# Convolution loop: one exponential instead of two, with an identity matmul that carries it to PSUM, and product buffers by step parity

## The chip, the core and the metric

The kernel runs on one core of a Trainium2 chip. The metric is the device time of one execution in microseconds (us); lower is better. The engines of the core are called TensorE (PE in the rows, its weight loads PEld), VectorE (DVE), ScalarE (ACT), GpSimd (POOL) and SyncE (SP). Each works through its own queue of instructions in order, and they meet only at semaphores.

## The reference

The whole kernel computes a convolution-like layer, then an attention layer, then a layer of experts. Only the first is touched. In it each output pixel is a sum over 49 neighbours, with weights that are a softmax over the neighbours:

```python
x1 = _conv1x1(x, w1c, b1c); x2 = _conv1x1(x, w2c, b2c); x3 = _conv1x1(x, w3c, b3c)
x2p = pad(x2, reflect)
diff = stack([x1 - x2p[:, :, dy:dy + H, dx:dx + W] for dy, dx in OFFS], axis=2)
y = relu(_bn(diff, bn1...)); y = einsum('bkln,ok->boln', y, cw1); y = relu(_bn(y, bn2...))
logits = einsum('bkln,ok->boln', y, cw2) + cw2_b
wgt = softmax(logits, axis=2)                 # over the 49 neighbours
for k, (dy, dx) in enumerate(OFFS):           # out: B, HN=8 heads, SP=8, H, W
    patch = x3p[:, :, dy:dy + H, dx:dx + W]
    out = out + patch * wgt[:, :, k]          # one weight for the 8 channels of a head
```

Shapes are B = 4 images, 64 channels, 56 x 56 pixels; the weights come from 32 channels (CR). All is float32.

## The kernel before

`conv_prepare` makes x1 and the padded x2 and x3. `conv_main`, where the change is, then works in 7 chunks of 8 rows (CH = 448 pixels). In a chunk the 49 neighbours are taken in STEPS = 14 steps of four or three neighbours (`taps`), so there are N = 98 steps. A partition of the wide tiles stands for an image, one of the (up to) four neighbours and a head.

The engines run through the same list of turns T. In one turn each engine does a piece of several steps, at fixed distances:

- POOL: `sub(T+1)` (x1 - x2 into `diff`, L411) and `shift` (logits minus their maximum, L418, in the ring `lg`), which is one step ahead of the exponentials.
- TensorE: `hidden(T)` (L596) into `ps_hid`; `sums(s-1, 1)` with s = T - 18; a rotation (L620) or the widening of the denominators (L627) in some turns; `logits(T-1)` (L611); `sums(s, 0)` (L642). `sums` adds the products of a step over its neighbours into `ps_acc`. Each product row has 448 pixels and behind them 56 columns (EXT) that hold the exponentials themselves, so that the same matmul adds up the softmax denominators.
- ScalarE: `exp_wide(s)` (L531) writes exp(logit) to the PSUM tile `ps_ev`; `front_relu(T+1)` (L510); `exp_ext(s)` (L535) computes the same 128x448 exponentials once more, into the EXT columns of the product tile (here called the edge exp); `hidden(T)` (L517); `logits(T-1)` (L522).
- VectorE: `running(T-2)` (L457, the running maximum); `product(s, 0)` and `product(s, 1)` (L477), the exponentials in `ps_ev` times the window of x3, for four channels each; `across` (L465) between the two products when a chunk's maximum is taken.

In turns T = 1 and 2 modulo 14 TensorE rotates the running maximum (L620, 128x448 against a 128*128 matrix) and the logits of that turn wait for `across`. In turns T = 4 modulo 14 ScalarE copies a finished chunk's sums out (L546, L547), and the first sums of the next chunk wait for it. In turns T = 5 modulo 14 VectorE takes the reciprocals (L493), ScalarE places them (L557), TensorE widens them (L627) and ScalarE copies the result (L564); the logits of that turn stand behind it. A turn later VectorE multiplies (L487).

`ps_ev` is one buffer: the wide exp of step s waits for `prod_done` of step s-1. The product tile `prod` is one buffer too (two halves `hs`): a product of step s waits for `acc_done` of the same half of step s-1. In the last 14 steps (s >= D0 = 84) `diff` and `ps_hid` are no longer in use, so a second product tile (`spare`) lies in `diff` and the wide exponentials rotate through the four banks of `ps_hid`, and POOL does a third of the products. SP brings a chunk's window of x3 (`win`) when the products of the chunk two before are done.

Of the kernel before, what the change touches and what calls it, by code (L numbers as in the profile page):

```python
# [26 lines left out]
NQ = 4  # L27
ROWS = 8
CH = ROWS * W
# [211 lines left out]
def conv_main(nc, x, cst, front, win, x3_dram, x3_sent, conv_out, tres_in, last_in, early_added):  # L241
    with ExitStack() as ctx:
        def sb(name, shape, dt=F32):
            return ctx.enter_context(nc.sbuf_tensor(name, shape, dt))
# [4 lines left out]
        def sem(name):  # L249
            return ctx.enter_context(nc.semaphore(name))  # L250

        QCH = CH // NQ
        EXT = QCH // 2
        ND, RING = 3, 18
        diff = sb("cm_diff", [128, ND, NQ, CH])
        hid = sb("cm_hid", [128, 2, B, CH])
        lg = sb("cm_lg", [128, RING, CH])
        prod = sb("cm_prod", [128, 2, NQ, CH + EXT])
        top = sb("cm_top", [128, 2, CH])
        topb = sb("cm_topb", [128, CH])  # L260
        rden_q = sb("cm_rden_q", [128, 2, EXT])
# [6 lines left out]
        ps_ev = psum("cm_ps_ev", [128, BANK])  # L268
# [9 lines left out]
        top_done = sem("cm_top_done")  # L278
        shift_done = sem("cm_shift_done")
        ev_done = sem("cm_ev_done")  # L280
        ext_done = sem("cm_ext_done")
        win_in = [sem(f"cm_win_in{a}") for a in range(2)]
        prod_done = sem("cm_prod_done")
# [19 lines left out]
        def mat(name, n=128):  # L303
            a = CONV_COLS[name][0]
            return cst[:, a:a + n]
# [5 lines left out]
        def step_at(T, d):  # L311

            return T - d if 0 <= T - d < N else None

        def chunk_at(T, d):
# [3 lines left out]

        D0 = N - STEPS  # L320
        SHIFTS_AHEAD = 6
        spare = diff[:, :, :, :].rearrange("p d q n -> p (d q n)")[:, 0:2 * NQ * (CH + EXT)] \
            .rearrange("p (h q n) -> p h q n", h=2, q=NQ)

        def by_pool(s, hs):

            return s >= D0 and (2 * (s - D0) + hs) % 3 == 1
# [8 lines left out]

        def halves_of(s):

            return spare if s >= D0 and (s - D0) % 2 == 0 else prod

        def wide_ev(s):

# [2 lines left out]
        def halves_free(eng, s, hs):  # L345


            if s == D0:
                eng.wait_ge(hid_done, N)
            elif s > D0:  # L350
                eng.wait_ge(acc_done, 2 * (s - 2) + hs + 1)
            elif s >= 1:
                eng.wait_ge(acc_done, 2 * (s - 1) + hs + 1)

        def window_of(s, hs):
            c, k = divmod(s, STEPS)
# [9 lines left out]
        with nc.Block() as block:  # L366
# [78 lines left out]
            @block.vector  # L445
            def _(v):
                def running(s):
                    c, k = divmod(s, STEPS)
                    v.wait_ge(logit_out, s + 1)
                    if k == 0:  # L450
                        if c >= 2:
                            v.wait_ge(rot_done, 2 * (c - 1))
                        v.tensor_scalar(top[:, c % 2, :], ps_lg[:, 0:CH], lane_bias(s), None,
                                        ALU.add).then_inc(run_done, 1)
                    else:
                        v.wait_ge(run_done, s)
                        v.scalar_tensor_tensor(out=top[:, c % 2, :], in0=ps_lg[:, 0:CH], scalar=lane_bias(s),  # L457
                                               in1=top[:, c % 2, :], op0=ALU.add, op1=ALU.max).then_inc(run_done, 1)

                def across(c, turn):  # L460

                    v.wait_ge(rot_done, 2 * c + turn + 1)
                    if turn == 1 and c >= 1:
                        v.wait_ge(shift_done, c * STEPS)
                    v.tensor_tensor(topb[:, :] if turn else top[:, c % 2, :], ps_lg[:, 0:CH], top[:, c % 2, :],  # L465
                                    ALU.max).then_inc(top_done, 1)

                def product(s, hs):
                    c, k = divmod(s, STEPS)
                    if by_pool(s, hs):  # L470
                        return
                    if k == 0 and hs == 0:
                        v.wait_ge(win_in[c % 2], 64 * (c // 2 + 1))
                    v.wait_ge(ev_done, s + 1)
                    halves_free(v, s, hs)
                    ev = wide_ev(s).unsqueeze(1).broadcast_to([128, 4, CH])
                    v.tensor_tensor(halves_of(s)[:, hs, :, 0:CH].rearrange("p s (r c) -> p s r c", c=W),  # L477
                                    ev.rearrange("p s (r c) -> p s r c", c=W), window_of(s, hs),
                                    ALU.mult).then_inc(prod_done, 1)

                v.memset(hid[96:128, 1, :, :], 0.0).then_inc(lanes_done, 1)
                v.memset(rden_d[:, :, :], 0.0).then_inc(lanes_done, 1)
                for T in TURNS:
                    c = chunk_at(T, MUL_D)
                    if c is not None:
                        v.wait_ge(wide_out, c + 1)
                        v.tensor_tensor(cout[:, :, :], cout[:, :, :],  # L487
                                        rden[:, :].unsqueeze(1).broadcast_to([128, 2, CH]),
                                        ALU.mult).then_inc(out_done, 1)
                    c = chunk_at(T, WIDE_D)  # L490
                    if c is not None:
                        v.wait_ge(acc_out, c + 1)
                        v.reciprocal(rden_q[:, :, :], rden_q[:, :, :]).then_inc(rden_done, 1)  # L493
                    if step_at(T, 2) is not None:
                        running(T - 2)
                    if step_at(T, SUM_D) is not None:
                        product(T - SUM_D, 0)
                    for turn, d in ((1, SECOND_TURN), (0, FIRST_TURN)):
                        c = chunk_at(T, d)
                        if c is not None:  # L500
                            across(c, turn)
                    if step_at(T, SUM_D) is not None:
                        product(T - SUM_D, 1)

            @block.scalar
            def _(act):
# [17 lines left out]

                def exp_wide(s):
                    act.wait_ge(shift_done, s + 1)
                    if s >= D0 + B:
                        act.wait_ge(prod_done, vector_halves(s - B, 1))
                    elif 1 <= s < D0:
                        act.wait_ge(prod_done, 2 * s)  # L530
                    act.activation(wide_ev(s), lg[:, s % RING, :], ACT.Exp).then_inc(ev_done, 1)  # L531

                def exp_ext(s):
                    halves_free(act, s, 1)
                    act.activation(halves_of(s)[:, :, :, CH:CH + EXT],  # L535
                                   lg[:, s % RING, :].rearrange("p (r h n) -> p h r n", h=2, n=EXT),
                                   ACT.Exp).then_inc(ext_done, 1)
                    if by_pool(s, 0) or by_pool(s, 1):
                        act.wait_ge(ext_done, s + 1)
                        act.activation(lg[:, s % RING, :], lg[:, s % RING, :], ACT.Exp).then_inc(flat_ev_done, 1)  # L540
# [23 lines left out]
                    act.copy(rden[:, :], ps_lg[:, 0:CH]).then_inc(wide_out, 1)  # L564

                for T in TURNS:
                    if step_at(T, SUM_D) is not None:
                        exp_wide(T - SUM_D)
                    if step_at(T, -1) is not None:
                        front_relu(T + 1)  # L570
                    c = chunk_at(T, WIDE_D)
                    if c is not None:
                        place(c)
                    if step_at(T, SUM_D) is not None:
                        exp_ext(T - SUM_D)
                    if step_at(T, 0) is not None:
                        hidden(T)
                    if c is not None:
                        widened(c)
                    c = chunk_at(T, OUT_D)  # L580
                    if c is not None:
                        sums_out(c)
                    if step_at(T, 1) is not None:
                        logits(T - 1)

            @block.tensor
            def _(pe):
# [43 lines left out]
                def sums(s, hs):  # L631
# [12 lines left out]
                                        tile_position=(0, 32 * r))  # L644
                    ins.then_inc(acc_done, 1)

                for T in TURNS:
                    if step_at(T, 0) is not None:
                        hidden(T)
                    if step_at(T, SUM_D + 1) is not None:  # L650
                        sums(T - SUM_D - 1, 1)
                    for turn, d in ((1, SECOND_TURN), (0, FIRST_TURN)):
                        c = chunk_at(T, d)
                        if c is not None:
                            rotate(c, turn)
                    c = chunk_at(T, WIDE_D)
                    if c is not None:
                        widen(c, T)
                    if step_at(T, 1) is not None:
                        logits(T - 1)  # L660
                    if step_at(T, SUM_D) is not None:
                        sums(T - SUM_D, 0)
# [1659 lines left out]
```

## Time and profile before

| | |
|---|---|
| median of 3 runs | 1947.26 us (1944.82 to 1948.8) |
| profiled execution, its own time | 1944.76 us |
| its span, first to last instruction | 1941.7 us |
| PE busy | 1695.3 us, 87% |
| DVE busy | 1198.4 us, 62% |
| ACT busy | 1176.5 us, 61% |
| POOL busy | 702.6 us, 36% |
| mean granted TensorE clock | 0.956 |

The span holds the convolution (to about 615 us), then attention, then the experts; busy shares are means over all three. In the rows a line gives the engine, the line of the kernel, the operation, the tiles written <- read and the shape; "x8" is a number of records that were merged, and the duration is then from the first one's start to the last one's end. A bracket tells how long the engine was idle before and which instruction ended it. Consecutive instructions of VectorE and ScalarE overlap by some 0.07 us in the records, so that the distance of two starts is a little less than a duration.

### The profile page before, as it was taken

The numbers are of one execution on the slowest core, as the hardware profiler recorded it, in microseconds if no ns is written. First come the engines' busy times: TensorE is split into PE (matmuls) and PEld (weight loads), VectorE is DVE, ScalarE is ACT, GpSimd is POOL, SyncE is SP. The second block draws the span as 40 slices with busy tenths as digits, with TensorE's granted clock in tenths as the row PEclk, the third lists the DMA queues.
The fourth block names the chain that finished last, engine by engine and source line by source line (L and its number), as shares of the span: only waits on it lengthen the run. The fifth ranks groups of instructions, "written<-read, shape, count | busy, mean of one in ns | idle before, by whom it ended". The sixth has DMA issues, their size and how long they took to land. (4 is left out here: it accounts for less than half of the span.)

```text
span 1941.7 us, 33831 instructions
## 1 busy us (share of the span) xinstructions
PE 1695.3 (87%) x13143; PEld 622.5 (32%) x13143; DVE 1198.4 (62%) x1798; ACT 1176.5 (61%) x1605; POOL 702.6 (36%) x401
## 2 busy tenths in 40 slices
PE   4468778778765789999999999999988999999998
PEld 1011111111111434433443443344343334433333
DVE  3239999999985576666666666666265445453433
ACT  3699999999942445454544454444464556566655
POOL 0798988988857310000000000000130114322222
PEclk9799999999987689999999999999997999999999
DMA  2121201211212210000000000100121000010000
GB/s 99 82 104 46 84 35 50 84 40 46 85 64 88 100 34 16 16 15 15 16 12 15 15 15 14 49 15 16 36 76 24 6 5 8 8 41 8 9 8 9
DMA packets 27712, 73.27 MB, mean 38 GB/s; under 512 B 6968, under 2 KB 16184, under 8 KB 26160
## 3 DMA queue, kind: packets, MB, share of 16 engines
q1 hardware_dynamic: 27280, 68.18, 11.0%
q10 hardware_dynamic: 288, 3.09, 0.4%
q8 instruction: 100, 1.64, 0.4%
q14 instruction: 44, 0.36, 0.1%
HBM read 47.84 MB, written 13.62 MB: 32 GB/s over the span
## 5 line engine op out<-in xcount | busy, mean ns | idle before, releaser
L1361 DVE TENSOR_REDUCE at_mpart<-at_ps_m 128x1 f32<-128x384 f32 (+3 forms) x800 | 396.4, 556 | 164.8 <-PE at_ps_m L1071 164.2
L1214 ACT ACTIVATE at_prob<-at_ps_s 128x896 f32<-128x896 f32 x336 | 305.0, 917 | 315.7 <-PE at_ps_s L1089 307.5
L411 POOL TENSOR_TENSOR cm_diff<-front 128x1792 f32<-128x1792 f32 x98 | 320.6, 3275 | 66.8 <-POOLq L113 37.6
L477 DVE TENSOR_TENSOR cm_prod<-cm_ps_ev,win 128x1792 f32<-128x1792 f32 x168 | 333.3, 2018 | 9.8 <-PE cm_ps_acc L642 5.2
L1906 ACT ACTIVATE ge_hid<-ge_ps,ffn 128x448 f32<-128x448 f32 x448 | 249.7, 634 | 122.6 <-PE ge_ps L1770 122.5
L1110 PE MATMUL at_ps_a<-at_prob,win 128*64 128x448 f32 x1344 | 290.0, 552 | 0.0
L1089 PE MATMUL at_ps_s<-vh,front 64*128 64x448 f16 x1344 | 252.1, 352 | 13.8 <-ACT at_prob L1214 7.8
L642 PE MATMUL cm_ps_acc<-cm_prod,cst 128*32 128x504 f32 x1456 | 200.0, 623 | 60.5 <-DVE cm_prod L477 27.0
L1089 PE MATMUL at_ps_s<-vl,front 64*128 64x448 f16 x1344 | 251.3, 351 | 0.0
L1009 POOL TENSOR_TENSOR attn<-attn 64x448 f32<-64x448 f32 x27 | 30.5, 1128 | 485.7 <-DMA attn<-attn 485.7
L1747 PE MATMUL ge_ps<-ge_hid,ffn 128*64 128x448 f32 x896 | 194.6, 555 | 0.5 <-DVE ge_part L2088 0.4
L517 ACT ACTIVATE cm_hid<-cm_ps_hid,cst 128x1792 f32<-128x1792 f32 x98 | 170.5, 1740 | 0.3 <-PE cm_ps_hid L596 0.3
L1071 PE MATMUL at_ps_m<-front,vh 64*128 64x384 f16 (+3 forms) x800 | 158.5, 338 | 10.5 <-DVE at_mpart L1361 9.0
L1770 PE MATMUL ge_ps<-attn,w1h 128*128 128x448 f16 (+1 forms) x448 | 160.9, 359 | 0.0
L1770 PE MATMUL ge_ps<-attn,w1l 128*128 128x448 f16 (+1 forms) x448 | 159.8, 357 | 0.0
L510 ACT ACTIVATE cm_diff<-cm_diff 128x1792 f32<-128x1792 f32 x98 | 147.5, 1505 | 13.7 <-POOL cm_diff L411 13.7
L596 PE MATMUL cm_ps_hid<-cm_diff,cst 32*32 32x448 f32 x2744 | 107.0, 577 | 53.5 <-ACT cm_hid L517 35.8
L2081 DVE COPY ge_wide<-ge_ps 128x448 f32<-128x448 f32 x112 | 69.9, 624 | 134.3 <-PE ge_ps L1760 133.8
L418 POOL TENSOR_TENSOR cm_lg<-cm_lg,cm_topb 128x448 f32<-128x448 f32 x98 | 115.5, 1184 | 48.8 <-DVE cm_topb L465 48.8
L2088 DVE SCALAR_TENSOR_TENSOR ge_part<-ge_ps,ffn,ge_wide 128x448 f32<-128x448 f32 x112 | 76.4, 682 | 77.5 <-PE ge_ps L1747 75.9
L2151 POOL TENSOR_TENSOR ge_total<-ge_part 128x448 f32<-128x448 f32 x28 | 32.1, 1146 | 246.9 <-DVE ge_part L2088 246.9
L1110 PEld LDWEIGHTS at_ps_a<-at_prob,win 128*64 128x64 f32 x1344 | 81.7, 136 | 122.9 <-issue 94.4
(232 smaller groups left out, 1964.4 us busy)
## 6 DMA issues: line engine op xcount, KB each, us to landing
win<-x_dram SPq DMA_DIRECT2D x28, 868.0 KB
at_rden<-rden_dram SPq DMA_DIRECT2D x27, 224.0 KB, 3.2
x_dram<-win SPq DMA_DIRECT2D x4, 962.0 KB
conv_out<-cm_cout SPq DMA_DIRECT2D x28, 112.0 KB, 3.6
win<-x SPq DMA_DIRECT2D x2, 1568.0 KB, 12.7
t_dram<-front SPq DMA_DIRECT2D x2, 1568.0 KB, 7.4
attn<-attn SPq DMA_DIRECT2D x28, 112.0 KB, 2.3
front<-t_dram SPq DMA_DIRECT2D x2, 1568.0 KB, 7.6
```

The source lines that it names most:

```text
L411: pool.tensor_tensor(diff[:, s % ND, 0:n, :].rearrange("p n (r c) -> p n r c", c=W), a.rearrange("p n (r c) -> p n r c", c=W), b, ALU.subt ...
L477: v.tensor_tensor(halves_of(s)[:, hs, :, 0:CH].rearrange("p s (r c) -> p s r c", c=W), ev.rearrange("p s (r c) -> p s r c", c=W), window_o ...
L517: act.activation(hid[0:n, s % 2, :, :], ps_hid[0:n, :, 0:CH], ACT.Relu, bias=vec("t2")[0:n]).then_inc(hrelu_done, 1)
L642: ins = pe.matmul(ps_acc[32 * r:32 * r + 32, hs, 0:CH + EXT], mat("tap_in", 32), halves_of(s)[:, hs, r, :], start=(k == 0), stop=(k == STE ...
L1071: pe.matmul(ps_m[0:w, j % RB, 0:n], queries, xs[rows, b, kb * KEYS:kb * KEYS + n], start=True, stop=True, tile_position=(64 * half, 0)).th ...
L1089: ins = pe.matmul(bank[:, a, :], xs[rows, m, at:at + TT], half[rows, m, columns_of(k)], start=(part + h == 0), stop=(part + h == 2), tile_ ...
L1110: ins = pe.matmul(ps_a[64 * a:64 * a + 64, at], xT[:, m // 2, key, 64 * i:64 * i + 64], moving, start=(s == 0), stop=(s == SL - 1), tile_p ...
L1214: act.activation(prob_of(s)[0:w, 0:a, :], ps_s[0:w, (s + 1 - par) % 2, 0:a, 0:CH], ACT.Exp).then_inc(exp_done, 1)
L1361: v.tensor_reduce(mpart[0:w, a, part:part + 1], ps_m[0:w, j % RB, 0:rough_columns(e)], AX.X, ALU.max).then_inc(rough_max, 1)
L1747: ins = pe.matmul(out_bank(b, k, ep)[64 * a:64 * a + 64, 0:CH], mat("w2", n, C), hid[:, j % NHB, :], start=(h == 0), stop=(h == 1), tile_p ...
L1770: ins = pe.matmul(hidden_bank(j)[:, 0:CH], w[:, n * 128:(n + 1) * 128], own16[b // 2][:, b % 2, columns_of(k)], start=(h == 0), stop=(h == 1))
L1906: act.activation(hid[:, j % NHB, :], hidden_bank(j)[:, 0:CH], ACT.Gelu, bias=mat("b1", n, 1)).then_inc(gelu_done, 1)
```

## The change

The wide exp is no longer done by ScalarE for the steps 0 to 83. ScalarE computes the exponentials once, into the EXT columns of the product tile (`exp_ext`, now the first piece of its turn). A new piece of TensorE, `move(s)`, multiplies these 448 columns with the identity matrix and so writes them to `ps_ev`. It stands in TensorE's turn behind `hidden(T)` and before `sums(s-1, 1)`. It waits for the exponentials (`ext_done`) and, as the wide exp did, for the products of the step before (`prod_done`). Products wait for it by a new semaphore, `ev_moved`.

The product tile is doubled and chosen by s % 2 in all steps, so that `spare` goes, and a product or edge exp of step s waits for `acc_done` of step s-2. The last 14 steps keep `exp_wide`, and count `ev_done` from there.

```diff
-        prod = sb("cm_prod", [128, 2, NQ, CH + EXT])
+        prod = sb("cm_prod", [128, 2, 2, NQ, CH + EXT])
...
         def halves_of(s):
-            return spare if s >= D0 and (s - D0) % 2 == 0 else prod
+            return prod[:, s % 2]
...
         def halves_free(eng, s, hs):
-            if s == D0:
-                eng.wait_ge(hid_done, N)
-            elif s > D0:
+            if s >= 2:
                 eng.wait_ge(acc_done, 2 * (s - 2) + hs + 1)
-            elif s >= 1:
-                eng.wait_ge(acc_done, 2 * (s - 1) + hs + 1)
...
-                    v.wait_ge(ev_done, s + 1)
+                    if s >= D0:
+                        v.wait_ge(ev_done, s - D0 + 1)
+                    else:
+                        v.wait_ge(ev_moved, s + 1)
...
                 def exp_wide(s):
                     act.wait_ge(shift_done, s + 1)
+                    if s == D0:
+                        act.wait_ge(hid_done, N)
                     if s >= D0 + B:
                         act.wait_ge(prod_done, vector_halves(s - B, 1))
-                    elif 1 <= s < D0:
-                        act.wait_ge(prod_done, 2 * s)
...
                 def exp_ext(s):
+                    act.wait_ge(shift_done, s + 1)
                     halves_free(act, s, 1)
...
-                    if step_at(T, SUM_D) is not None:
-                        exp_wide(T - SUM_D)
+                    s = step_at(T, SUM_D)
+                    if s is not None and s >= D0:
+                        exp_wide(s)
+                    elif s is not None:
+                        exp_ext(s)
...
+                def move(s):
+
+                    pe.wait_ge(ext_done, s + 1)
+                    if s >= 1:
+                        pe.wait_ge(prod_done, 2 * s)
+                    pe.matmul(ps_ev[:, 0:CH], mat("ident"),
+                              halves_of(s)[:, :, :, CH:CH + EXT].rearrange("p h r n -> p r h n"), start=True,
+                              stop=True).then_inc(ev_moved, 1)
+
                 for T in TURNS:
                     if step_at(T, 0) is not None:
                         hidden(T)
+                    if step_at(T, SUM_D) is not None and T - SUM_D < D0:
+                        move(T - SUM_D)
                     if step_at(T, SUM_D + 1) is not None:
                         sums(T - SUM_D - 1, 1)
```

## Rows read from the trace of the kernel before

**Rows 1.** Windows of the conv's middle: engine busy us and records, granted clock (PEclk), DMA.

```profile
460.00:470.00 10.00, 8.17 (x116) 1.83 (x108) 9.63 (x7) 9.70 (x12) 9.30 (x5) 1.00 0.01 2
...
420.00:424.00 4.00, 2.57 (x20) 0.45 (x32) 3.04 (x4) 4.00 (x7) 3.58 (x2) 0.62 0.26 100
```

**Rows 2.** VectorE timeline, plain turns: start us, duration, engine, line, operation, idle before it.

```profile
439.78 0.69 DVE L457 SCALAR_TENSOR_TENSOR cm_top<-cm_ps_lg,cst,cm_top 128x448 f32<-128x448 f32 x1
...
449.25 0.68 DVE L457 SCALAR_TENSOR_TENSOR cm_top<-cm_ps_lg,cst,cm_top 128x448 f32<-128x448 f32 x1 [0.29 <-ACT cm_lg L522]
...
449.85 3.95 DVE L477 TENSOR_TENSOR cm_prod<-cm_ps_ev,win 128x1792 f32<-128x1792 f32 x2
...
468.18 0.69 DVE L457 SCALAR_TENSOR_TENSOR cm_top<-cm_ps_lg,cst,cm_top 128x448 f32<-128x448 f32 x1 [0.29 <-ACT cm_lg L522]
```

**Rows 3.** Timeline of all engines, same plain turns, ScalarE and one weight load.

```profile
448.60 0.62 ACT L522 ACTIVATE cm_lg<-cm_ps_lg,cst 128x448 f32<-128x448 f32 x1
...
449.11 0.53 ACT L531 ACTIVATE cm_ps_ev<-cm_lg 128x448 f32<-128x448 f32 x1
...
449.58 1.32 ACT L510 ACTIVATE cm_diff<-cm_diff 128x1344 f32<-128x1344 f32 x1
...
451.32 1.74 ACT L517 ACTIVATE cm_hid<-cm_ps_hid,cst 128x1792 f32<-128x1792 f32 x1
...
451.98 0.19 PEld L642 LDWEIGHTS cm_ps_acc<-cm_prod,cst 128*32 128x32 f32 x8 [1.25 <-ACT cm_prod L535]
...
453.89 0.55 ACT L531 ACTIVATE cm_ps_ev<-cm_lg 128x448 f32<-128x448 f32 x1 [0.30 <-DVE cm_prod L477]
```

**Rows 4.** Timeline of two turns with a rotation, chunk end near 402 to 409 us.

```profile
401.68 2.02 DVE L477 TENSOR_TENSOR cm_prod<-cm_ps_ev,win 128x1792 f32<-128x1792 f32 x1
...
403.62 0.61 DVE L465 TENSOR_TENSOR cm_top<-cm_ps_lg,cm_top 128x448 f32<-128x448 f32 x1
...
404.35 0.19 PEld L611 LDWEIGHTS cm_ps_lg<-cm_hid,cst 128*32 128x32 f32 x8 [1.80 <-issue]
...
406.11 0.24 PEld L596 LDWEIGHTS cm_ps_hid<-cm_diff,cst 32*32 32x32 f32 x32 [0.82 <-ACT cm_hid L517]
...
407.08 0.17 PEld L642 LDWEIGHTS cm_ps_acc<-cm_prod,cst 128*32 128x32 f32 x8 [0.73 <-issue]
...
408.07 0.30 PEld L620 LDWEIGHTS cm_ps_lg<-cm_top,cst 128*128 128x128 f32 x2 [0.83 <-issue]
...
409.13 0.62 DVE L465 TENSOR_TENSOR cm_topb<-cm_ps_lg,cm_top 128x448 f32<-128x448 f32 x1 [0.27 <-PE cm_ps_lg L620]
```

**Rows 5.** Timeline of two turns in which a chunk's sums go out, 420 to 430 us.

```profile
420.45 0.92 ACT L547 COPY cm_cout<-cm_ps_acc 128x896 f32<-128x896 f32 x1
...
421.42 0.20 PEld L642 LDWEIGHTS cm_ps_acc<-cm_prod,cst 128*32 128x32 f32 x8 [3.34 <-ACT cm_cout L547]
...
422.18 0.58 DVE L457 SCALAR_TENSOR_TENSOR cm_top<-cm_ps_lg,cst,cm_top 128x448 f32<-128x448 f32 x1
...
423.83 1.15 ACT L557 COPY cm_rden_d<-cm_rden_q 32x112 f32<-32x112 f32 x4
...
427.93 0.52 ACT L564 COPY cm_rden<-cm_ps_lg 128x448 f32<-128x448 f32 x1
...
428.49 0.16 PEld L611 LDWEIGHTS cm_ps_lg<-cm_hid,cst 128*32 128x32 f32 x8 [2.53 <-ACT cm_rden L564]
...
430.19 0.68 DVE L457 SCALAR_TENSOR_TENSOR cm_top<-cm_ps_lg,cst,cm_top 128x448 f32<-128x448 f32 x1 [0.56 <-ACT cm_lg L522]
...
430.23 0.25 PEld L596 LDWEIGHTS cm_ps_hid<-cm_diff,cst 32*32 32x32 f32 x32 [0.82 <-issue]
```

**Rows 6.** One line's instructions, L620 and L477: durations min/median/max, first and last start.

```profile
L620 PE MATMUL cm_ps_lg<-cm_top,cst x28: 539/643/1116, 122.0 to 552.7; 128*128 128x448 f32 x28
...
L477 DVE TENSOR_TENSOR cm_prod<-cm_ps_ev,win x168: 2014/2015/2026, 134.1 to 558.8; 128x1792 f32<-128x1792 f32 x168
...
L477 DVE TENSOR_TENSOR cm_diff<-cm_ps_hid,win x9: 2014/2015/2025, 560.8 to 604.8; 128x1792 f32<-128x1792 f32 x9
```

More of the change, by code:

```diff
@@ L280, in conv_main @@
         ev_done = sem("cm_ev_done")
+        ev_moved = sem("cm_ev_moved")
         ext_done = sem("cm_ext_done")
@@ L321, in conv_main @@
         SHIFTS_AHEAD = 6
-        spare = diff[:, :, :, :].rearrange("p d q n -> p (d q n)")[:, 0:2 * NQ * (CH + EXT)] \
-            .rearrange("p (h q n) -> p h q n", h=2, q=NQ)
         def by_pool(s, hs):
@@ L573, in _ @@
                         place(c)
-                    if step_at(T, SUM_D) is not None:
-                        exp_ext(T - SUM_D)
+                    if s is not None and s >= D0:
+                        exp_ext(s)
                     if step_at(T, 0) is not None:
```

## Prediction

> **What bounds the kernel now.** I read the page first for the stage, then windows over it, then the timeline of a plain stretch and of the two kinds of irregular turn, and last the totals of single lines. All edits lie in the convolution's main loop. I call one value of T a turn. The 84 turns that are changed (steps 0 to 83) run from the first product at 134.1 us to the first product that takes its exponentials from `ps_hid`, at 560.8 us [rows 6]: 426.7 us. Everything after this is a block of its own and moves with it.
>
> In the middle of the stage VectorE and ScalarE are both above 9.6 of 10 us, POOL is at 9.3 and TensorE at 8.2, with TensorE's clock fully granted, 2.4 GHz [rows 1]. VectorE's `running` starts at 439.78 and, six turns later, at 468.18 [rows 2]: 28.40 / 6 = 4.73 us a turn. VectorE alone would need less: 0.60 us from `running` to the first product and 3.95 us for the two products, some 4.5 us. Its gap (0.29 us, every second turn, [rows 2]) ends with ScalarE's logits. ScalarE in turn has hardly a gap of its own: logits, wide exp, relu, edge exp, hidden follow each other, and where it does stop (0.30 us) the wide exp waits for the last product to give `ps_ev` free [rows 3]. So a turn costs 4.73 us because ScalarE's five pieces and VectorE's three are tied together at this one buffer; TensorE is off the path. The 0.55 us of the wide exp lie beside VectorE's `running`, so from the end of a product to the next turn's first product only about 0.6 us pass.
>
> **The change, part by part.** Times are start to start where one instruction follows another.
>
> *Wide exp removed.* 84 times 0.55 us on ScalarE [rows 3], 46 us of work. That takes ScalarE from 4.7 to some 4.2 us a turn. By itself this could bring the turn to VectorE's 4.5 us, a gain of at most 0.2 us x 84, about 19 us. It is a gain only if nothing else is above 4.5.
>
> *Product buffer by step parity.* In a plain turn no product waits for `acc_done` now [rows 2], so this buys nothing there. It does at a chunk end: sums start at 421.42, 3.34 us late, after ScalarE's copy of the sums [rows 5], and the next step's products had to wait for them. In the last 14 steps two buffers existed already (`spare` and `prod`), and their rule of waiting is the same. No queue of SP is moved.
>
> *Exponentials moved by TensorE.* The 84 `move` matmuls have the shape of the rotation on L620: full 128*128 array, 448 fp32 columns, recorded as two weight loads and two matmuls. A rotation's weight load starts at 408.07 and VectorE, waiting for it, starts at 409.13 [rows 4]: 1.06 us from start to use. That is the price I take. Its bounds are 0.65 us (the shortest of one recorded matmul of it, 0.54, [rows 6], plus 0.11 us of hand-over) and 2.1 us (1.06 doubled: the longest record of it, 1.12, is about double the others, [rows 6], which is the 1.2 GHz level). The move's input is read in eight pieces of 56 columns, which no row of this size shows; I take that as free, with the 2.1 as its bound as well. Between the ends I go by the rotation, since it is the same instruction pair with the same kind of waiter.
>
> A rule of the Trainium skill gives less. The Trainium skill (TensorE: Matmul & The Clock Gate, Single matmul latency) gives (398 + N)/2.4 ns for one bf16 matmul at full clock, and the Trainium skill (FP8 and Floating Point Precision) counts four passes for true fp32; taken together as 4 x 448 columns this is an estimate of 0.91 us, which would lower the sum below by 84 x 0.15 = 13 us. The row holds the weight load and the hand-over as well, so the row stays.
>
> Two chains now go through the move, and both can be added up.
>
> Chain A, VectorE and TensorE. `move(s)` waits `prod_done` of the step before, as `ps_ev` is still single. From the first product to the end of the second 3.95 us [rows 2], hand-over to TensorE 0.11 (product start 449.85 plus 2.02 gives 451.87, the weight load starts at 451.98, [rows 2, 3]), move 1.06: 5.12 us. `running` (0.68 us) lies inside and no longer hides the whole turnaround.
>
> Chain B, TensorE in order. Queued ahead of the move are `sums(s-1, 0)` and `hidden(T)`. Product start to sums' weight load 2.13 [rows 2, 3], `hidden` to the next load 0.97 (406.11 to 407.08), sums to the next load 0.98 (407.08 to 408.07) [rows 4], move 1.06: 5.14 us. Nothing on ScalarE stretches this: its `hidden` is over some 1.3 us after the product's start and is wanted at 3.1.
>
> Both give 5.13 us against 4.73. TensorE's work in a turn (sums 2 x 0.98, hidden 0.97, logits 1.76 - 0.98 = 0.78 by the 404.35 and 406.11 rows [rows 4], move about 1.0) is 4.7, so it fits. Behind the waiting move stand `sums(s-1, 1)` and the logits; they have 3.2 us until the first product ends and need 2.8. POOL, at 9.3 us in a window of over two turns, fits too [rows 1].
>
> *Rotation turns.* Logits wait for `across`, which VectorE does after the first product: product 401.68, across 403.62, logits' weight load 404.35, hidden 406.11, next load 407.08 [rows 4]. Before, nobody hurried for this. Now the move stands behind it: 407.08 - 401.68 = 5.40, plus 1.06 = 6.46 us. There are 10 such turns with logits.
>
> *Turns in which the denominators are placed.* By the order of its pieces (copy of the sums 0.92, logits 0.62, edge exp, relu) I put the end of ScalarE's relu, or the reciprocal that `place` waits for, at 0.2 us before the turn's product start; place takes 1.15 [rows 5], hidden 1.7, the copy 0.52, so the logits go at +3.17; hidden comes 1.74 later (428.49 to 430.23, [rows 5]), the move 0.97 after, the product 1.06 after: 6.9 us. There are 5. VectorE's reciprocal and its product with the denominators fit in. Before, this turn took 8.0 us (422.18 to 430.19, [rows 5]), since the copy of the sums had held the products. So here about 1 us a chunk comes back, and 0.4 to 0.8 in the turn before, in which ScalarE now has room for the copy.
>
> *Last four turns.* No hidden and no logits: 5.13, twice plus 0.53 for `across`, and I add 1.6 us in all because TensorE idles there and its rotation's records double to 1.12 us [rows 6], the 1.2 GHz level; a clock of 0.62 also stands in a gap at a chunk end [rows 1]. Sum 23.2.
>
> Sum: 65 x 5.13 + 10 x 6.46 + 5 x 6.9 + 23.2 = 333.5 + 64.6 + 34.5 + 23.2 = 455.8 us, against 426.7: **29 us more**. The profiled execution took 1944.8 us (span 1941.7 and 3.1 around it), 2.5 below the median of 1947.3; on the median it makes 1976 us, 1.5% slower.
>
> **Rivals.**
>
> *The move hides (faster).* If the result were at VectorE 0.65 us after its release, near the time that `running` takes anyway, chain A falls to 4.71 and chain B to 4.73. Each of the 84 turns gives 0.41 us back, 34 us: 421 us, 5 less than now, or about 1942; the chunk ends' gain is then what is left. It decides at a move of 1.06 - 29/84 = 0.72 us. For it: one matmul's record is 0.54. Against it: there are two, and the rotation that VectorE waits for shows 1.06 [rows 4].
>
> *No difference.* The same with a move of 0.67 to 0.77 us, or chunk ends that give back over 4 us each: 1947.
>
> *The move is slow.* Pieces of 56 columns or the 1.2 GHz level in every turn: 2.1 us, 1.04 x 84 = 87 us on top: 2063, and with half the turns 2020. For it: more waits in a ring through TensorE. Against it: TensorE will work over 9 tenths of each turn, and it kept its full clock at 8 tenths [rows 1].
>
> *Order on TensorE binds less than I think.* In the rows TensorE's work comes in the order of its queue [rows 4], and that makes chain B and the rotation turns. If only chain A held, a rotation turn would be 5.12 + 0.53 = 5.65 us and the sum 10 x 0.81 = 8 us smaller: 1968, inside the forecast. The Trainium skill (PSUM: Partial Sum Buffer, Engine vs sequencer instructions) states that matmuls start and complete in program order, which is the row's side.
>
> **How the numbers follow.** Forecast 0.76; the move hides 0.07; no difference 0.05; slow move 0.12. The forecast's own range is from 21 less (a move 0.15 shorter, a third of the way to its lower bound, 13 us; and the 8 of the queue's order) to 20 more (0.24 us a turn of hand-overs that I did not count): 1955 to 1996. The first two rivals lie below it and hold 12 in 100; of the slow ones a mild case (a fifth of the turns at 2.1) is taken in by going to 2000. Range 1955 to 2000. About 0.2%, 4 us, is what this measurement tells from no change. Slower 0.88, same 0.05, faster 0.07.
>
> **What would show it.** After: the move 1.05 us from weight load to product; VectorE idle about 0.5 us before each first product, ended by TensorE; plain turns of 5.13; rotation turns near 6.5; the sums' 3.3 us gap at a chunk end gone; ScalarE at some 83% in the stage and idle before hidden and logits. It would be wrong if the product follows `running` without a gap, if the two chains' hand-overs are 0.1 us more or less each (8 us a piece), or if TensorE's clock falls in plain turns.

## The result and the profile after

The changed kernel takes 1975.15 us (median of 4 runs, 1974.39 to 1975.87) against 1946.04 us of the kernel before (4 runs). The ratio is 1.0152, 95% interval 1.0131 to 1.0173: slower by 29 us, where 1976 was forecast. The profiled execution has a span of 1974.1 us.

First the stage as a whole. The product's line in the changed kernel is L474. Its totals (durations min/median/max in ns, first and last start):

```profile
L474 DVE TENSOR_TENSOR cm_prod<-cm_ps_ev,win x168: 2014/2020/2026, 135.2 to 587.7; 128x1792 f32<-128x1792 f32 x168
...
L474 DVE TENSOR_TENSOR cm_prod<-cm_ps_hid,win x19: 1961/2016/2026, 589.7 to 639.2; 128x1792 f32<-128x1792 f32 x19
```

The 84 changed turns last from 135.2 to 589.7, 454.5 us, against 426.7 [rows 6] and a forecast of 455.8. That is 27.8 us of the difference of the two spans, 32.4. The stage starts 1.1 us later, as the first product now waits for edge exp and move; the last 14 steps, from 589.7 to the last product at 639.2, are 0.9 us shorter. The other 4.4 us lie in later stages whose code is the same, and one kernel's runs differ by more than that (before: 1941.34 to 1948.8), so they are given no cause here.

The same views as in [rows 1] and [rows 2]. Windows of the changed kernel (busy us and number of records of TensorE, its weight loads, VectorE, ScalarE, POOL; then the granted clock):

```profile
460.00:470.00 10.00, 9.05 (x108) 2.12 (x104) 8.77 (x7) 8.07 (x9) 8.45 (x5) 1.00 0.45 138
...
420.00:558.00 138.00, 123.42 (x1390) 30.05 (x1366) 120.13 (x85) 110.27 (x115) 109.39 (x52) 1.00 0.17 60
```

TensorE is now the busiest at 9.05 of 10 us, VectorE has fallen from 9.63 to 8.77 and ScalarE from 9.70 to 8.07. No engine is full: the time is lost in a ring of waits. The clock is 1.00 over the whole 138 us, chunk ends included.

Plain turns, VectorE:

```profile
456.72 3.96 DVE L474 TENSOR_TENSOR cm_prod<-cm_ps_ev,win 128x1792 f32<-128x1792 f32 x2 [0.60 <-PE cm_ps_ev L653]
...
460.60 0.68 DVE L451 SCALAR_TENSOR_TENSOR cm_top<-cm_ps_lg,cst,cm_top 128x448 f32<-128x448 f32 x1
...
461.90 3.96 DVE L474 TENSOR_TENSOR cm_prod<-cm_ps_ev,win 128x1792 f32<-128x1792 f32 x2 [0.63 <-PE cm_ps_ev L653]
...
492.88 3.96 DVE L474 TENSOR_TENSOR cm_prod<-cm_ps_ev,win 128x1792 f32<-128x1792 f32 x2 [0.63 <-PE cm_ps_ev L653]
```

From 456.72 to 492.88 are seven turns: 5.17 us each (before 4.73). In each of them VectorE stands idle behind `running` for 0.60 or 0.63 us, until TensorE's L653, the move, is done.

One plain turn of all engines:

```profile
451.58 3.96 DVE L474 TENSOR_TENSOR cm_prod<-cm_ps_ev,win 128x1792 f32<-128x1792 f32 x2 [0.90 <-PE cm_ps_ev L653]
...
453.72 0.19 PEld L643 LDWEIGHTS cm_ps_acc<-cm_prod,cst 128*32 128x32 f32 x8 [1.25 <-issue]
...
454.73 0.21 PEld L597 LDWEIGHTS cm_ps_hid<-cm_diff,cst 32*32 32x32 f32 x24 [0.82 <-issue]
...
455.67 0.30 PEld L653 LDWEIGHTS cm_ps_ev<-cm_prod,cst 128*128 128x128 f32 x2 [0.73 <-issue]
```

Product at 451.58, sums' weight load 2.14 later, hidden 1.01 later, move 0.94 later, next product at 456.72, 1.05 later: 5.14 us. The second product ends at 451.58 + 3.96 = 455.54, and with the 0.11 us of hand-over the move could start at 455.65; it starts at 455.67. In this turn the two chains reach the move at the same moment.

Rotation turns (L621 rotates, L459 is `across`):

```profile
421.52 2.02 DVE L474 TENSOR_TENSOR cm_prod<-cm_ps_ev,win 128x1792 f32<-128x1792 f32 x1 [0.60 <-PE cm_ps_ev L653]
...
427.98 2.02 DVE L474 TENSOR_TENSOR cm_prod<-cm_ps_ev,win 128x1792 f32<-128x1792 f32 x1 [1.38 <-PE cm_ps_ev L653]
...
434.41 3.96 DVE L474 TENSOR_TENSOR cm_prod<-cm_ps_ev,win 128x1792 f32<-128x1792 f32 x2 [1.35 <-PE cm_ps_ev L653]
...
439.65 3.96 DVE L474 TENSOR_TENSOR cm_prod<-cm_ps_ev,win 128x1792 f32<-128x1792 f32 x2 [0.69 <-issue]
```

The two rotation turns take 6.46 and 6.43 us, the next one 5.24.

The chunk end:

```profile
441.79 0.19 PEld L643 LDWEIGHTS cm_ps_acc<-cm_prod,cst 128*32 128x32 f32 x8 [1.30 <-ACT cm_cout L545]
...
444.80 3.96 DVE L474 TENSOR_TENSOR cm_prod<-cm_ps_ev,win 128x1792 f32<-128x1792 f32 x2
...
447.80 0.16 PEld L612 LDWEIGHTS cm_ps_lg<-cm_hid,cst 128*32 128x32 f32 x8 [1.83 <-ACT cm_rden L562]
...
450.52 0.30 PEld L653 LDWEIGHTS cm_ps_ev<-cm_prod,cst 128*128 128x128 f32 x2 [0.73 <-ACT cm_prod L533]
```

TensorE's gap before the sums, which ScalarE's copy ends, is now 1.30 us and not 3.34 [rows 5]. In the plain turn above it is 1.25 (453.72), so the copy delays next to nothing any more; the turn before takes 5.15 us (439.65 to 444.80) and the place turn 6.78 (444.80 to 451.58).

The last turns that have a move, and the first product without one:

```profile
574.48 2.02 DVE L474 TENSOR_TENSOR cm_prod<-cm_ps_ev,win 128x1792 f32<-128x1792 f32 x1 [0.58 <-PE cm_ps_ev L653]
...
580.14 2.02 DVE L474 TENSOR_TENSOR cm_prod<-cm_ps_ev,win 128x1792 f32<-128x1792 f32 x1 [1.17 <-PE cm_ps_ev L653]
...
585.80 3.96 DVE L474 TENSOR_TENSOR cm_prod<-cm_ps_ev,win 128x1792 f32<-128x1792 f32 x2 [1.17 <-PE cm_ps_ev L653]
...
589.68 2.01 DVE L474 TENSOR_TENSOR cm_prod<-cm_ps_hid,win 128x1792 f32<-128x1792 f32 x1
```

Both rotation turns take 5.66 us, which is the 5.65 of chain A with `across` (no hidden and no logits stand in them). The last turn takes only 3.88, for the product behind it needs no move. The granted clock stayed at 1.00 here:

```profile
574.00:584.00 10.00, 7.40 (x40) 1.58 (x38) 8.35 (x6) 1.21 (x3) 1.22 (x2) 1.00 0.00 0
```

### The profile page after: what moved, and what is told of

Its sections match the earlier page's. It is cut to its first block and busy times, and to the rows that moved or that the text cites. A ratio compares the mean times of both kernels' runs of the same rounds, so it can differ in the third digit from the quotient of the medians.

```text
span 1974.1 us, 34178 instructions
## 1 busy us (share of the span) xinstructions
PE 1758.8 (89%) x13311; PEld 644.1 (33%) x13311; DVE 1197.6 (61%) x1798; ACT 1140.2 (58%) x1521; POOL 698.3 (35%) x401
## 5 line engine op out<-in xcount | busy, mean ns | idle before, releaser
L474 DVE TENSOR_TENSOR cm_prod<-cm_ps_ev,win 128x1792 f32<-128x1792 f32 x168 | 333.3, 2020 | 59.3 <-PE cm_ps_ev L653 55.9
L643 PE MATMUL cm_ps_acc<-cm_prod,cst 128*32 128x504 f32 x1568 | 210.2, 617 | 52.8 <-DVE cm_prod L474 35.1
L597 PE MATMUL cm_ps_hid<-cm_diff,cst 32*32 32x448 f32 x2744 | 102.0, 554 | 36.9 <-ACT cm_hid L514 20.7
```

Of the source, the lines that this page charges most:

```text
L643: ins = pe.matmul(ps_acc[32 * r:32 * r + 32, hs, 0:CH + EXT], mat("tap_in", 32), halves_of(s)[:, hs, r, :], start=(k == 0), stop=(k == STE ...
```

## Experiments

I compare the kernels by their medians and by the length of the 84 turns in the profile (first product to first product from `ps_hid`). Every kernel was run beside the kernel before, whose medians were 1946.86 us (first four) and 1945.98 us (the rest).

| kernel | median us | ratio to before, 95% interval | 84 turns, us |
|---|---|---|---|
| before | 1946.0 | | 426.7 |
| changed | 1975.15 | 1.0152 (1.0131 to 1.0173) | 454.5 |
| doubled tile only | 1939.42 | 0.9962 (0.9947 to 0.9976) | 421.5 |
| changed, no move | 1919.68 | 0.9858 (0.9843 to 0.9873) | 400.2 |
| changed, half a move | 1945.28 | 0.9994 (0.9982 to 1.0007) | 425.5 |
| changed, move first | 1979.73 | 1.0166 (1.0149 to 1.0182) | 461.9 |
| changed, move late | 2058.33 | 1.0578 (1.0557 to 1.0599) | 539.0 |
| the same, single tile | 2149.77 | 1.1048 (1.1022 to 1.1074) | 633.5 |
| SBUF and PSUM in turn | 2056.26 | 1.0563 (1.0545 to 1.058) | 535.4 |
| products read SBUF | 2184.37 | 1.1222 (1.1202 to 1.1242) | 656.3 |

### The doubled product tile alone

```diff
 (kernel before)
-        prod = sb("cm_prod", [128, 2, NQ, CH + EXT])
+        prod = sb("cm_prod", [128, 2, 2, NQ, CH + EXT])
...
-            return spare if s >= D0 and (s - D0) % 2 == 0 else prod
+            return prod[:, s % 2]
...
-            if s == D0:
-                eng.wait_ge(hid_done, N)
-            elif s > D0:
+            if s >= 2:
                 eng.wait_ge(acc_done, 2 * (s - 2) + hs + 1)
-            elif s >= 1:
-                eng.wait_ge(acc_done, 2 * (s - 1) + hs + 1)
```

> The kernel before with the product tile doubled by parity and nothing else (both exponentials stay on ScalarE). My theory: plain turns stay at 4.73 us, since no product waits for the sums there; the gain lies in the five chunk ends, where the next products and the edge exp no longer wait for the late sums, about 1 us each: 1941 us against 1946. Rival: ScalarE's waits for the sums before the edge exp (11 us in the waits of before) count in full, in plain turns too: 1930. If the doubling buys nothing at all: 1946.

Measured 1939.42 us, 7 us less; the 84 turns are 5.2 us shorter. Of this 4.3 us lie in the five chunk ends, 0.3 to 1.7 us in each, and 0.9 in the last turns before step 84. VectorE's timeline of this kernel:

```profile
415.56 0.68 DVE L451 SCALAR_TENSOR_TENSOR cm_top<-cm_ps_lg,cst,cm_top 128x448 f32<-128x448 f32 x1 [0.29 <-ACT cm_lg L516]
...
432.97 0.67 DVE L451 SCALAR_TENSOR_TENSOR cm_top<-cm_ps_lg,cst,cm_top 128x448 f32<-128x448 f32 x1
...
437.96 0.68 DVE L451 SCALAR_TENSOR_TENSOR cm_top<-cm_ps_lg,cst,cm_top 128x448 f32<-128x448 f32 x1 [0.29 <-ACT cm_lg L516]
...
447.43 0.69 DVE L451 SCALAR_TENSOR_TENSOR cm_top<-cm_ps_lg,cst,cm_top 128x448 f32<-128x448 f32 x1 [0.29 <-ACT cm_lg L516]
```

From 437.96 to 447.43, two plain turns, 9.47 us, as before. From 415.56 (the turn in which sums go out) to 432.97, three turns on, 17.41 us; in the kernel before the same stretch is 18.50, from 416.61 on its timeline to 435.11. One turn further on (437.96 here, 439.78 before) 0.8 us of the 1.1 are left, since plain turns last 4.46 and 5.00 us alternately in both kernels. So the gain is at the chunk ends, and the waits of the edge exp in other turns were worth nothing.

### No move, and half a move

```diff
 (changed kernel: no move)
-                    if step_at(T, SUM_D) is not None and T - SUM_D < D0:
+                    if T - SUM_D == 0:
                         move(T - SUM_D)
...
-                        v.wait_ge(ev_moved, s + 1)
+                        v.wait_ge(ev_moved, 1)
+                        v.wait_ge(ext_done, s + 1)
```

> The changed kernel with the move left out for all steps but the first: the products of steps 1 to 83 take the exponentials of step 0 from PSUM, as soon as the edge exp of their own step is done. My theory: the whole loss and more is the move's place on the path, so plain turns fall from 5.16 to VectorE's 4.5 us, rotation turns from 6.45 to 5.0; about 65 us less, 1910. Rival: ScalarE's relief is worth nothing since POOL (4.45 us a turn) or the hidden ring holds the turn near 4.7: 1930. Rival: the loss is not the move but the doubled tile or the reordered ScalarE: it stays at 1960 or more.

```diff
 (changed kernel: half a move)
+                    n = NQ // 2 if s else NQ
-                    pe.matmul(ps_ev[:, 0:CH], mat("ident"),
-                              halves_of(s)[:, :, :, CH:CH + EXT].rearrange("p h r n -> p r h n"), start=True,
+                    pe.matmul(ps_ev[:, 0:n * QCH], mat("ident"),
+                              halves_of(s)[:, :, 0:n, CH:CH + EXT].rearrange("p h r n -> p r h n"), start=True,
                               stop=True).then_inc(ev_moved, 1)
```

> The changed kernel with the move of steps 1 to 83 cut to half its columns (224 of 448; the other half of the wide exponentials stays that of step 0). My theory: what counts is the time from the move's start to its result, in both chains, and streaming is 0.75 of its 1.06 us. 0.37 us less in each of 84 turns: plain turns 4.79, 31 us less, 1944. Rival: the fixed part (weight loads, hand-over) is most of it: 0.15 us a turn less, 1962.

Neither kernel computes the right result: the products take exponentials of step 0, all of them or half. They are there for the time alone.

Without the move 1919.68 us, 55 less than the changed kernel. VectorE's timeline:

```profile
408.37 3.94 DVE L475 TENSOR_TENSOR cm_prod<-cm_ps_ev,win 128x1792 f32<-128x1792 f32 x2
...
412.47 2.34 DVE L485 TENSOR_TENSOR cm_cout<-cm_cout,cm_rden 128x896 f32<-128x896 f32 x1 [0.15 <-ACT cm_rden L563]
...
415.34 3.94 DVE L475 TENSOR_TENSOR cm_prod<-cm_ps_ev,win 128x1792 f32<-128x1792 f32 x2
...
424.46 3.95 DVE L475 TENSOR_TENSOR cm_prod<-cm_ps_ev,win 128x1792 f32<-128x1792 f32 x2
...
428.92 3.95 DVE L475 TENSOR_TENSOR cm_prod<-cm_ps_ev,win 128x1792 f32<-128x1792 f32 x2
```

428.92 - 424.46 = 4.46 us a plain turn, no wait: VectorE alone. So the relief is real. But this kernel drops two things at once: the second exponential, and the wait of the writer of `ps_ev` for the last product. It doesn't tell how much either is worth. It is also 10 us slower than the expected 1910. The turn with the denominators' product takes 6.97 us (408.37 to 415.34), 2.34 of them in that product (L485), which lasts 1.09 us in the half-move kernel. In the other chunks L485 takes 2.2 to 3.5 us. Its two inputs lie in SBUF, and the last experiment shows what that costs beside POOL. The second rotation turn also still waits (5.52 us).

With half a move 1945.28 us. VectorE's timeline:

```profile
436.27 3.96 DVE L474 TENSOR_TENSOR cm_prod<-cm_ps_ev,win 128x1792 f32<-128x1792 f32 x2 [0.23 <-PE cm_ps_ev L654]
...
474.60 2.02 DVE L474 TENSOR_TENSOR cm_prod<-cm_ps_ev,win 128x1792 f32<-128x1792 f32 x1 [0.23 <-PE cm_ps_ev L654]
```

Eight turns in 38.33 us, 4.79 each, as expected to the hundredth; 30 us less than the changed kernel for 84 x 0.37 = 31. From the weight load of the half move to the product are 0.69 us (449.97 to 450.66). So what the move costs is its own duration, streaming above all, and it is paid in every turn.

Four numbers now close the account for the 84 turns: doubled tile -5.2 (426.7 to 421.5), one exponential less on ScalarE and no wait of its writer at `ps_ev` -21.3 (421.5 to 400.2), the move with its wait for the last product +54.3 (400.2 to 454.5). Sum +27.8.

### The place of the move in TensorE's queue

```diff
 (changed kernel: move first; for "late" it stands behind sums(T - SUM_D - 1, 1))
                 for T in TURNS:
+                    if step_at(T, SUM_D) is not None and T - SUM_D < D0:
+                        move(T - SUM_D)
                     if step_at(T, 0) is not None:
                         hidden(T)
-                    if step_at(T, SUM_D) is not None and T - SUM_D < D0:
-                        move(T - SUM_D)
```

> The changed kernel with the move ahead of hidden in TensorE's turn. My theory, both chains bind in a plain turn: the order chain loses 0.97 us, the product chain stays, so plain turns stay at 5.13 to 5.16; rotation turns fall from 6.45 to 5.5 and place turns from 6.8 to 5.8. 15 us less, 1960 us. Rival, only the order binds: plain turns fall as well, towards VectorE's 4.5, and the kernel comes to about 1910.

> The changed kernel, two product tiles, with the move behind the sums of the step before in TensorE's turn. My theory: both chains through the move grow by one sums group, 0.95 to 0.98 us a turn, plain turns of 6.1: 2056. Rival: TensorE has slack there and the move's place is of no account: 1975 to 1985.

Move first: 1979.73 us. The expected 15 us less did not come; it is 5 us more. VectorE's timeline:

```profile
425.90 2.02 DVE L474 TENSOR_TENSOR cm_prod<-cm_ps_ev,win 128x1792 f32<-128x1792 f32 x1 [0.58 <-PE cm_ps_ev L653]
...
428.77 0.62 DVE L459 TENSOR_TENSOR cm_top<-cm_ps_lg,cm_top 128x448 f32<-128x448 f32 x1 [0.84 <-PE cm_ps_lg L621]
...
432.76 2.02 DVE L474 TENSOR_TENSOR cm_prod<-cm_ps_ev,win 128x1792 f32<-128x1792 f32 x1 [0.85 <-PE cm_ps_ev L653]
...
450.73 3.96 DVE L474 TENSOR_TENSOR cm_prod<-cm_ps_ev,win 128x1792 f32<-128x1792 f32 x2 [0.66 <-PE cm_ps_ev L653]
...
457.70 3.96 DVE L474 TENSOR_TENSOR cm_prod<-cm_ps_ev,win 128x1792 f32<-128x1792 f32 x2 [0.62 <-PE cm_ps_ev L653]
...
462.83 3.96 DVE L474 TENSOR_TENSOR cm_prod<-cm_ps_ev,win 128x1792 f32<-128x1792 f32 x2 [0.58 <-PE cm_ps_ev L653]
...
467.96 3.96 DVE L474 TENSOR_TENSOR cm_prod<-cm_ps_ev,win 128x1792 f32<-128x1792 f32 x2 [0.58 <-PE cm_ps_ev L653]
```

The timeline of all engines of the same kernel, in its place turn:

```profile
456.02 0.57 ACT L533 ACTIVATE cm_prod<-cm_lg 128x448 f32<-128x448 f32 x1
...
456.64 0.30 PEld L653 LDWEIGHTS cm_ps_ev<-cm_prod,cst 128*128 128x128 f32 x2 [1.27 <-ACT cm_prod L533]
```

Plain turns are 5.13 us (467.96 - 462.83): with the order chain out of the way, the product chain alone holds the turn, at the 5.12 that was added up for it. So the rival, that only the order binds, is false: order was worth 0.04 us in plain turns (5.17 to 5.13). The error was in the rotation turns: 6.86 us (425.90 to 432.76) and not 5.5. The rotation stands behind hidden in the queue, and hidden now behind the move, so the rotation itself is late: VectorE waits 0.84 us for it before `across`, with the logits behind that. What the move then waits for is a third path, which the expectation left out: ScalarE's edge exp stands behind the logits in ScalarE's queue. In the rotation turn it runs from 431.08 to 431.65, and the move starts at 431.70. The place turn (6.97) is late for the same reason (456.02, 456.64). One piece moved forward moved three back.

Move late: 2058.33 us, plain turns of 6.15 us, 84.5 us more in the 84 turns, 1.0 a turn: the sums group that stands ahead. As expected (2056). What stands between the end of the products and the move is paid in full.

### Single product tile with the late move

```diff
 (late move, and)
-            return prod[:, s % 2]
+            return prod[:, 0 if s < D0 else 1 - (s - D0) % 2]
...
-            if s >= 2:
+            if s > D0:
                 eng.wait_ge(acc_done, 2 * (s - 2) + hs + 1)
+            elif 1 <= s < D0:
+                eng.wait_ge(acc_done, 2 * (s - 1) + hs + 1)
```

> The changed kernel with the product tile single again (as before, with its second place in the last 14 steps only); the move then has to stand behind the sums of the step before, which it now needs. My theory: from the end of a product to the next come sums 1.16, edge exp 0.6, move 1.06 and hand-overs, some 3.0 us in place of 1.2: plain turns of 6.95, 150 us more than the changed kernel, 2125. Rival: the edge exp is early enough anyway and only the queue place counts: as the kernel with the late move and two tiles, about 2056.

Measured 2149.77 us; all engines, one turn:

```profile
401.40 0.17 PEld L645 LDWEIGHTS cm_ps_acc<-cm_prod,cst 128*32 128x32 f32 x8 [0.73 <-DVE cm_prod L476]
...
402.58 0.58 ACT L535 ACTIVATE cm_prod<-cm_lg 128x448 f32<-128x448 f32 x1 [2.66 <-PE cm_ps_acc L645]
...
403.21 0.30 PEld L655 LDWEIGHTS cm_ps_ev<-cm_prod,cst 128*128 128x128 f32 x2 [1.64 <-ACT cm_prod L535]
...
404.27 3.95 DVE L476 TENSOR_TENSOR cm_prod<-cm_ps_ev,win 128x1792 f32<-128x1792 f32 x2 [2.44 <-PE cm_ps_ev L655]
```

Sums at 401.40, edge exp at 402.58, move at 403.21, product at 404.27: one after another, after products that end at 401.2. Plain turns are 6.97 us (6.95 expected), but the whole is 25 us above the expected 2125: the irregular turns are longer than was allowed for, 7.5 to 9.8 us. This is what the second tile does in this change: not a gain by itself, but the condition for the edge exp to run ahead of the move.

### Products that read the exponentials from SBUF

If the move is the cost and one exponential the gain, the products could read the edge columns where they are. Two kernels tried SBUF as the source.

```diff
 (kernel before with the doubled tile: PSUM in even steps, SBUF in odd ones)
+        evs = sb("cm_evs", [128, CH])
...
-            return ps_hid[:, s % B, 0:CH] if s >= D0 else ps_ev[:, 0:CH]
+            if s >= D0:
+                return ps_hid[:, s % B, 0:CH]
+            return evs[:, :] if s % 2 else ps_ev[:, 0:CH]
...
-                    elif 1 <= s < D0:
-                        act.wait_ge(prod_done, 2 * s)
+                    elif 2 <= s < D0:
+                        act.wait_ge(prod_done, 2 * (s - 1))
```

> The kernel before with the doubled product tile, no move, both exponentials on ScalarE, and the wide ones written to the PSUM tile in even steps and to an SBUF tile in odd ones, so that the wide exp no longer waits for the products just ahead. My theory: the tie through the one buffer goes, ScalarE runs its five pieces back to back, plain turns of 4.6 instead of 4.73, 10 us less than with the doubled tile alone, 1929. Rival: a product that takes both inputs from SBUF is slower, or POOL is slower beside it: 2.02 us grows and nothing or less than nothing is left, 1940 or more.

```diff
 (changed kernel, no move; tile with the inner dimensions swapped)
-        prod = sb("cm_prod", [128, 2, 2, NQ, CH + EXT])
+        prod = sb("cm_prod", [128, 2, NQ, 2, CH + EXT])
...
-                        v.wait_ge(ev_moved, s + 1)
+                        v.wait_ge(ext_done, s + 1)
...
+                        ev = prod[:, s % 2, :, :, CH:CH + EXT].rearrange("p q h n -> p (q h) n") \
+                            .unsqueeze(1).broadcast_to([128, 4, ROWS, W])
```

> The changed kernel without the move and with no PSUM copy at all in steps 0 to 83: exponentials computed once, and the products read them from the product tile's own edge columns in SBUF (the tile's two inner dimensions are swapped so that these columns form one pattern). Everything is computed. My theory: like the kernel without the move, VectorE's 4.46 us a turn, 1920. Rival: both inputs from SBUF cost VectorE or POOL time: each 0.1 us a product is 17 us, 1937 and up.

2056.26 and 2184.37 us: both far slower, by the rival. Groups of instructions by form, from 230 to 500 us of the alternating kernel (busy us, mean ns):

```profile
L474 DVE TENSOR_TENSOR cm_prod<-cm_evs,win 128x1792 f32<-128x1792 f32 x42 | 150.6, 3619 | 0.0
...
L474 DVE TENSOR_TENSOR cm_prod<-cm_ps_ev,win 128x1792 f32<-128x1792 f32 x41 | 81.0, 2008 | 0.0
...
L408 POOL TENSOR_TENSOR cm_diff<-front 128x1792 f32<-128x1792 f32 x21 | 100.2, 4769 | 11.3 <-PE cm_ps_hid L595 11.3
```

The same product takes 2008 ns from PSUM and 3619 ns from SBUF in one kernel, and POOL's subtraction 4769 ns where it was about 3720. In the direct kernel, VectorE and POOL:

```profile
343.91 2.01 DVE L478 TENSOR_TENSOR cm_prod<-cm_prod,win 128x1792 f32<-128x1792 f32 x1
```

```profile
333.13 2.93 POOL L412 TENSOR_TENSOR cm_lg<-cm_lg,cm_topb 128x448 f32<-128x448 f32 x1
336.02 5.49 POOL L405 TENSOR_TENSOR cm_diff<-front 128x1792 f32<-128x1792 f32 x1
...
346.53 2.87 POOL L412 TENSOR_TENSOR cm_lg<-cm_lg,cm_topb 128x448 f32<-128x448 f32 x1 [5.02 <-DVE cm_topb L459]
```

At 343.91 the SBUF product takes 2.01 us: POOL's subtraction of 336.02 has ended at 341.51 and it starts nothing until 346.53, so the source by itself costs nothing. Over 230 to 500 us the same line takes 3.57 us in the mean, and POOL's shift 2.93 us instead of 1.16. The two engines hold each other up when both take their inputs from SBUF. The Trainium skill (SBUF: State Buffer, SBUF: two separate sides) describes this as one pair of ports that VectorE, with two SBUF inputs, and POOL lock in turn for a whole instruction; the trace agrees, with about 1.77 us added to either of POOL's instructions. With products from SBUF both kernels are 110 us or more slower than the kernel before; so in this kernel the exponentials are better read from PSUM, and a single exponential into SBUF needs something that carries it there.

## Why the prediction was right

- *What bounds a plain turn before* (ScalarE and VectorE tied at `ps_ev`): shown in part. Without the second exponential, the move and the wait at `ps_ev` it is VectorE's 4.46 us (4.5 stated). The relief over all 84 turns was 21.3 us, against "at most 19" for the plain rate alone; irregular turns have a share. What the shared buffer costs by itself no kernel shows: the one that was to show it (SBUF and PSUM in turn) met the slower products.
- *Doubled tile worth nothing in plain turns, something at chunk ends*: shown, 9.47 us for two turns with and without it, 0.3 to 1.7 us a chunk.
- *The move at 1.06 us, the rotation's price*: 1.05 (455.67 to 456.72). The eight pieces of 56 columns cost nothing to be seen. The estimate of 0.91 us by the Trainium skill (TensorE: Matmul & The Clock Gate, Single matmul latency; FP8 and Floating Point Precision, TensorE Precision Notes) was too low by 0.14; the row decided rightly.
- *Chain A 5.12, chain B 5.14*: 5.13 with the order out of the way, 5.17 with both. In chain B sums to hidden took 1.01 in place of 0.98, and `hidden` 0.94 and 0.97 alternately, which gives turns of 5.14 and 5.17 or 5.18.
- *Rotation turns 6.46*: 6.46 and 6.43, with the move's weight load 5.40 us behind the product as added up (421.52 to 426.92). *Place turns 6.9*: 6.78.
- *Last four turns 23.2*: this term was mis-sized. It measured 20.3 (5.13 for the first, 5.66 twice, 3.88). I had added 1.6 us for TensorE at 1.2 GHz, and the clock stayed full; and I had charged the last turn with a move, where the next product takes none.
- Plain turns (65 of 5.166 in place of 5.13) were 2.3 us more and the last four 2.9 less, so the sum, 455.8 against 454.5, is closer than its terms. That the medians meet the forecast to 1 us is luck in part: the two profiled spans differ by 32.4 us and not 29, and the runs of the kernel before spread over 7.5 us.
- *The move hides*: false, the move would have to be near 0.7 us. The half move, with 0.69, came out at 0.9994 of the kernel before: it lies close to the turning point of 0.72 that the prediction gave.
- *Slow move*: false, the clock was 1.00 in the whole stage. *Order binds less*: false in plain turns, where both chains agree within 0.04 us. In rotation turns the order does bind, but by less than the 0.81 us that the rival gave it. There the edge exp runs from 425.77 to 426.34 and the move, behind hidden, starts at 426.92, so without the order the path over logits and edge exp would still take some 5.9 us, an estimate from these rows. The prediction didn't price this path.

## What to carry to other kernels

A piece of work that is taken off a busy engine and put on an idle one is paid by what it adds between the end of one turn's last consumer and the start of the next turn's first, not by busy shares: here 0.55 us beside other work became 1.06 us in the path, because both the single buffer that it fills and the order of the queue put it behind the last product. No kernel gave `ps_ev` a second buffer; by the sums above chain B alone would still hold a plain turn at 5.14. Add up each ring (buffer and queue order) in start-to-start times before moving anything, irregular turns apart; a piece moved forward in an in-order queue moves all that it passes back. When an exotic route (here through PSUM) looks avoidable, look first at which two engines would then read the same memory. Of the kernels tried, the doubled tile alone, with both exponentials on ScalarE, is the fastest that computes everything: 0.9962 of the kernel before.

## What was not expected of the hardware

- VectorE and POOL with SBUF inputs at the same time: 2.01 us became 3.6 us, 1.16 became 2.93. The products of the kernel before take one input from PSUM, but its trace does show the effect once a chunk, where VectorE multiplies by the denominators and POOL's shift takes 2.00 us:

```profile
428.47 1.16 DVE L487 TENSOR_TENSOR cm_cout<-cm_cout,cm_rden 128x896 f32<-128x896 f32 x1 [0.57 <-ACT cm_rden L564]
...
428.65 2.00 POOL L418 TENSOR_TENSOR cm_lg<-cm_lg,cm_topb 128x448 f32<-128x448 f32 x1
```

- TensorE's granted clock rose with the change: around the chunk end's gap it had a mean of 0.62 over 4 us [rows 1], so most of them at 1.2 GHz. After the change TensorE is 8.9 tenths busy over 420 to 558 us, its gap there is 1.30 us in place of 3.34, and the clock stayed at 2.4 GHz. The 454.5 us hold whatever this gave back; no run separates it.
